# A routed expert layer and a gated recurrence on one core: gathers without pace, down products one unit sooner, and a new layout of the recurrence's pieces

## The reference

```python
shared = silu(xf @ w1) * (xf @ w3) @ w2
s = sigmoid(concat([xf, tf]) @ router_W)              # tf: cond, repeated over the tokens
topk_idx = top_k(s + router_bias, 2); gates = s of the two / their sum
y = gelu(xf @ W1e[e]) @ W2e[e]                        # for each expert e
x = x + (shared + sum of gates * y over the two) / 3
# then, from h = cond, for t in 0..255:
gate = sigmoid(h @ Wh.T + x[:, t] @ Wz.T + b)
h = tanh(h * (1 - alpha) + gate * x[:, t])
out[:, t] = x[:, t] + h
```

## Time and profile before

| | us |
|---|---|
| median of 3 runs | 763.66 |
| lowest, highest | 762.21, 768.95 |
| the profiled execution, its own time | 764.96 |
| its span, first to last instruction | 763.1 |

### The profile page before, as it was taken

One profiled execution on the slowest core, in us unless ns is written; L12 is line 12 of the kernel. 1 busy time (PEld: TensorE's weight loads), 2 busy tenths in 40 slices (PEclk: granted clock), 3 DMA queues, 4 the chain that ended last, 5 costly groups with the idle time before them and its releaser, 6 DMA issues.

```text
span 763.1 us, 22288 instructions
## 1 busy us (share of the span) xinstructions
PE 700.4 (92%) x8562; PEld 505.6 (66%) x8562; DVE 547.1 (72%) x2014; ACT 472.9 (62%) x1347; POOL 270.8 (35%) x284
## 2 busy tenths in 40 slices
PE   5899897998999999999999899999999999999763
PEld 3455486645888656898578786566889555686442
DVE  4887651457877698877688786898976678866854
ACT  4746473634677755777676577556877645676533
POOL 2037464265642156452174025773040173002100
PEclk9999998999999999999999999999999999999965
DMA  8836899893896785996869654366475354133101
GB/s 284 326 112 228 220 247 263 204 201 109 208 237 191 166 166 146 216 203 186 208 152 224 112 140 158 127 164 142 105 202 140 113 153 132 43 92 118 43 15 43
DMA packets 166460, 124.73 MB, mean 163 GB/s; under 512 B 118706, under 2 KB 147156, under 8 KB 166356
## 3 DMA queue, kind: packets, MB, share of 16 engines
q1 hardware_dynamic: 150436, 79.19, 44.7%
q0 software_dynamic: 14368, 41.96, 17.3%
q10 hardware_dynamic: 1552, 2.15, 0.8%
HBM read 39.90 MB, written 55.84 MB: 125 GB/s over the span
## 4 chain that ended last, share of the span: by engine, by line
PE 68%; DVE 15%; ACT 8%; DMA 4%; issue 3%; POOL 0%; ACTq 0%; DVEq 0%; POOLq 0%
PE bank L1739 64%; PE bank L1967 2%; DVE hid_low L1507 2%; DVE pre L1561 2%; DMA xe<-x_slots_even 2%; DVE taken L1558 2%; DVE full L1500 1%; PE bank L1902 1%; DMA y_got<-y_slots_even,where 1%; ACT th L1257 1%; ACT hs_high L1265 1%; DVE r_part L1522 1%; DVE r_sum L1526 1%; DVE left L1419 1%; DVE x_parts L1378 1%
## 5 line engine op out<-in xcount | busy, mean ns | idle before, releaser
L1739 PE MATMUL bank<-xe,w1e_high 128*128 128x128 f16 x1360 | 215.9, 221 | 9.5 <-DMA xe<-x_slots_even 5.9
L1739 PE MATMUL bank<-xs,w_high 128*128 128x512 f16 x512 | 167.3, 382 | 5.2 <-DVE w_low L1677 3.0
L1739 PE MATMUL bank<-xe,w1e_low 128*128 128x128 f16 x680 | 146.9, 221 | 1.1
L1739 PEld LDWEIGHTS bank<-xe,w1e_high 128*128 x1360 | 125.5, 99 | 20.9 <-issue 7.8
L1507 DVE TENSOR_TENSOR hid_low<-full,hid_high 128x512 f16<-128x512 f32 (+1 forms) x152 | 102.9, 677 | 49.2 <-ACT hid_high L1210 39.1
L1257 ACT ACTIVATE th<-bank 128x64 f32<-128x64 f32 x256 | 56.9, 222 | 93.3 <-PE bank L1739 89.5
L1265 ACT ACTIVATE hs_high<-pre 128x64 f16<-128x64 f32 x256 | 65.5, 256 | 73.1 <-DVE pre L1561 64.8
L1558 DVE SCALAR_TENSOR_TENSOR taken<-th,zq 128x64 f32<-128x64 f32 x256 | 57.9, 226 | 69.7 <-ACT th L1257 66.8
L1739 PEld LDWEIGHTS bank<-hs_high,gwt_high 128*128 128x128 f16 x1024 | 68.2, 97 | 51.8 <-ACT hs_high L1265 38.0
L1078 POOL TENSOR_TENSOR fence_pool<-zero 128x1 f32<-128x1 f32 x12 | 3.4, 280 | 274.7 <-DMA y_slots_odd<-y_pair 84.7
L1739 PE MATMUL bank<-hs_high,gwt_high 128*128 128x32 f16 x1024 | 79.1, 178 | 20.5 <-ACT hs_high L1265 20.0
(11 more groups left out here) (156 smaller groups left out, 1704.4 us busy)
## 6 DMA issues: line engine op xcount, KB each, us to landing
y_slots_even<-y_pair SPq DMA_DIRECT2D x45, 256.0 KB
y_slots_odd<-y_pair SPq DMA_DIRECT2D x37, 256.0 KB
x_res<-in_x_dram SPq DMA_DIRECT2D x16, 512.0 KB
out_dram<-o_tok SPq DMA_DIRECT2D x32, 256.0 KB, 3.5
x_tok<-in_x_dram SPq DMA_DIRECT2D x14, 512.0 KB
x_slots_even<-zeros POOLq DMA_DIRECT2D x1, 4096.0 KB, 18.1
x_slots_odd<-zeros POOLq DMA_DIRECT2D x1, 4096.0 KB, 15.0
y_got<-in_L_cond_W1e_dram SPq DMA_DIRECT2D x4, 512.0 KB, 13.9
```

Of the source, the lines that this page charges most:

```text
L1739: return pe.matmul(out_ap, w, mov, start=start, stop=stop, skip_group_check=True)
```

## The change

Nothing that is computed changes, and each engine's instructions stay the same in kind and number but for their waits. What changes is where they stand:

- GATHER_STEP of sections 3 and 4 is -1 throughout: no pace. (Section 2 keeps its own.) The last scatters of section 4 are paced by steps 109 to 134 where it was 112 to 143, those of section 5 by steps 149 to 154 where it was 163 to 170. GATHER_AT and SCATTER_AT move by some units; the gathers of section 3 begin one unit sooner in POOL's order, among the scatters of section 4.
- The down products of the units in SOON stand one unit after their up products, where it was two. Where a unit then has two, both are done, one behind the other; where it has none, it has none.
- act_residual follows: one unit sooner for groups 12 and 13.
- Group 12's second transposes (kc = 1) stand in the same unit 133 as its first, behind the down products (LATE). Before, they stood in 134 and 135.
- FINISH moves for group 12 (132 to 131), 13 (135 stays) and 14 (138 to 141). Group 15's four tiles are weighed in two units again, where it was one.
- OUT_AT moves some chunks by one to four units, for instance chunk 22 from 128 to 130.
- PE_AT, ACT_AT and DVE_AT are new from unit 42 on.

```diff
-FINISH = [FIRST_SHARED[_q] + GROUP for _q in range(N_GROUPS)]
-for _q, _u in enumerate((37, 40, 43, 61, 64, 67, 83, 86, 89, 104, 107, 111, 132, 135, 138, 151)):
-    FINISH[_q] = _u
-AT_ONCE = (15,)
-SUM_AT = {_q: [FINISH[_q] + 2 - (_q in AT_ONCE), FINISH[_q] + 3 - (_q in AT_ONCE)] for _q in range(N_GROUPS) if AHEAD[_q]}
...
+FINISH = [37, 40, 43, 61, 64, 67, 83, 86, 89, 104, 107, 111, 131, 135, 141, 151]
+AT_ONCE = ()
+SUM_AT = [[39, 40], [42, 43], [45, 46], [63, 64], [66, 67], [69, 70], [85, 86], [88, 89], [91, 92], [106, 107], [109, 110], [113, 114], [133, 133], [137, 138], [143, 145], [152, 153]]
+SOON = (100, 110, 128, 129, 131, 132, 133, 134, 135, 138, 150)
...
-SCATTER_AT = [[_f + _j * _a // _b for _j in range(_n)] for _n, _f, _a, _b in zip(
-    SECTIONS, (7, 18, 39, 63, 96, 118), (1, 1, 1, 1, 2, 1), (2, 1, 1, 1, 3, 1))]
-GATHER_AT = [[_f + _j * _a // _b for _j in range(_n)] for _n, _f, _a, _b in zip(
-    SECTIONS, (34, 58, 80, 100, 128, 148), (1, 1, 1, 1, 1, 1), (2, 2, 2, 2, 2, 2))]
+SCATTER_AT = [
+    [7, 7, 8, 8, 9, 9, 10, 10, 11, 11, 12, 12], [18, 19, 20, 21, 22, 23, 24, 25, 26, 27, 28, 29],
+    [39, 40, 41, 42, 43, 44, 45, 46, 47, 48, 49, 50], [63, 64, 65, 66, 67, 68, 69, 70, 71, 72, 73, 74],
+    [96, 96, 97, 98, 98, 99, 100, 100, 101, 102, 102, 103], [109, 110, 111, 112],
+]
+GATHER_AT = [
+    [34, 34, 35, 35, 36, 36, 37, 37, 38, 38, 39, 39], [58, 58, 59, 59, 60, 60, 61, 61, 62, 62, 63, 63],
+    [80, 80, 81, 81, 82, 82, 83, 83, 84, 84, 85, 85], [99, 99, 100, 100, 101, 101, 102, 102, 103, 103, 104, 104],
+    [135, 135, 136, 136, 137, 137, 138, 138, 139, 139, 140, 140], [147, 147, 148, 148],
+]
...
-    4: (112, 113, 114, 115, 116, 117, 118, 119, 120, 121, 122, 123, 126, 127, 128, 129, 132, 133, 136, 137, 138, 139, 142, 143),
-    5: (163, 164, 165, 166, 167, 168, 169, 170),
+    4: (109, 110, 111, 112, 113, 114, 115, 116, 117, 118, 119, 120, 123, 124, 125, 120, 123, 124, 127, 128, 129, 130, 133, 134),
+    5: (149, 150, 151, 152, 153, 154, 154, 149),
...
-    3: (123, 124, 125, 125, 129, 130, 131, 131, 133, 134, 135, 135, 139, 140, 140, 141, 143, 144, 144, 145, 146, 146, 147, 148),
-    4: (187, 187, 188, 188, 189, 189, -1, -1, 191, -1, -1, -1, -1, -1, -1, -1, -1, -1, -1, -1, -1, -1, -1, 192),
+    3: (-1, -1, -1, -1, -1, -1, -1, -1, -1, -1, -1, -1, -1, -1, -1, -1, -1, -1, -1, -1, -1, -1, -1, -1),
+    4: (-1, -1, -1, -1, -1, -1, -1, -1, -1, -1, -1, -1, -1, -1, -1, -1, -1, -1, -1, -1, -1, -1, -1, -1),
...
-    46: 0, 49: 1, 53: 2, 57: 3, 61: 4, 70: 5, 71: 6, 73: 7, 78: 8, 82: 9, 92: 10, 94: 11, 97: 12, 98: 13, 100: 14,
-    104: 15, 111: 16, 115: 17, 118: 18, 119: 19, 120: 20, 123: 21, 128: 22, 132: 23, 138: 24, 141: 25, 147: 26,
-    150: 27, 153: 28, 154: 29, 155: 30, 156: 31,
+    46: 0, 49: 1, 53: 2, 57: 3, 61: 4, 70: 5, 71: 6, 73: 7, 78: 8, 82: 9, 92: 10, 94: 11, 97: 12, 99: 13, 100: 14,
+    104: 15, 111: 16, 115: 17, 118: 18, 121: 19, 122: 20, 125: 21, 130: 22, 133: 23, 138: 24, 141: 25, 147: 26,
+    150: 27, 154: 28, 157: 29, 159: 30, 160: 31,
...
     assert _u not in MISC, (_u, _item)
     MISC[_u] = _item
-SPARE = [MISC[_u] for _u in sorted(MISC)]
+LATE = {_at[0]: (SUM, (_q, 1)) for _q, _at in enumerate(SUM_AT) if _at[1] == _at[0]}
+SPARE = [_at[_u] for _u in sorted(MISC) for _at in (MISC, LATE) if _u in _at]
+assert all(UNITS[_u].kind == SHARED == UNITS[_u + 1].kind for _u in SOON)
...
 
+        def down_at(i):
+
+            return i + DOWN_LAG - (i in SOON)
+
...
-                    if u.i == (FIRST_SHARED[q] + MID + DOWN_LAG if AHEAD[q] else max(FIRST_SHARED[q] + MID, FINISH[q]) + 2):
+                    if u.i == (down_at(FIRST_SHARED[q] + MID - 1) + 1 if AHEAD[q] else max(FIRST_SHARED[q] + MID, FINISH[q]) + 2):
...
-                        if AHEAD[q] and u.i == SUM_AT[q][kc]:
+                        if AHEAD[q] and u.i == SUM_AT[q][kc] and (kc == 0 or u.i not in LATE):
                             add_part(q, kc)
                             gap()
                 gap()
                 if u.kind == SHARED:
                     product(u)
+                if u.i in LATE:
+                    gap()
+                    add_part(*LATE[u.i][1])
...
                         turn_tokens(q)
-                pair_down, shared_down = units_at(u.i - DOWN_LAG, EXPERT), units_at(u.i - DOWN_LAG, SHARED)
-                if shared_down and u.kind != SHARED:
-                    down_shared(shared_down, gap)
+                pair_down = units_at(u.i - DOWN_LAG, EXPERT)
+                shared_downs = [units_at(i, SHARED) for i in range(u.i - DOWN_LAG, u.i)
+                                if units_at(i, SHARED) and down_at(i) == u.i]
+                if shared_downs and u.kind != SHARED:
+                    down_shared(shared_downs[0], gap)
                 gap()
                 if u.kind == EXPERT:
...
+                    for v in shared_downs:
+                        if v is not shared_downs[0]:
+                            gap()
+                        down_shared(v, gap)
                     gap()
+                if u.i in LATE:
+                    misc(*LATE[u.i], gap)
```

The tables where the steps of group 12 begin and where the ordinary work ends, PE's part:

```diff
...
-    (131, 2): ((HIGH, 188),), (131, 3): ((STEP, 188),), (131, 10): ((HIGH, 189),), (131, 11): ((STEP, 189),),
-    (132, 0): ((HIGH, 190),), (132, 1): ((STEP, 190),), (132, 8): ((HIGH, 191),), (132, 9): ((STEP, 191),),
...
-    (136, 7): ((FILL, 48), (FILL, 49), (HIGH, 192), (STEP, 192),), (136, 14): ((HIGH, 193), (STEP, 193),),
...
-    (151, 18): ((HIGH, 231), (STEP, 231), (FILL, 58), (FILL, 59), (HIGH, 232), (STEP, 232),),
-    (152, 5): ((HIGH, 233), (STEP, 233),), (152, 7): ((HIGH, 234), (STEP, 234), (HIGH, 235),), (152, 9): ((STEP, 235),),
-    (153, 5): ((HIGH, 236), (STEP, 236), (HIGH, 237),), (153, 6): ((STEP, 237),),
...
+    (132, 8): ((HIGH, 187), (STEP, 187),), (132, 16): ((HIGH, 188), (STEP, 188),), (132, 25): ((HIGH, 189),),
+    (133, 1): ((STEP, 189),), (133, 11): ((HIGH, 190), (STEP, 190),), (133, 21): ((HIGH, 191), (STEP, 191),),
+    (134, 11): ((FILL, 48), (FILL, 49), (HIGH, 192), (STEP, 192), (FILL, 50), (FILL, 51), (HIGH, 193), (STEP, 193),),
+    (134, 17): ((HIGH, 194),), (134, 18): ((STEP, 194),), (135, 7): ((HIGH, 195), (STEP, 195),),
...
+    (151, 14): ((HIGH, 231),), (151, 15): ((STEP, 231), (FILL, 58), (FILL, 59), (HIGH, 232), (STEP, 232),),
+    (151, 20): ((HIGH, 233),), (151, 21): ((STEP, 233),), (151, 26): ((HIGH, 234),), (152, 0): ((STEP, 234),),
+    (152, 3): ((HIGH, 235),), (152, 5): ((STEP, 235),), (153, 5): ((HIGH, 236), (STEP, 236), (HIGH, 237),),
+    (153, 6): ((STEP, 237),), (154, 0): ((HIGH, 238), (STEP, 238),),
...
```

More of the change, by code:

```diff
@@ L358 @@
+    (159, 5): ((GATE, 251), (STATE, 251), (GATE, 252),),
+    (160, 4): ((STATE, 252), (GATE, 253), (STATE, 253), (GATE, 254),), (161, 3): ((STATE, 254),),
+    (161, 4): ((GATE, 255),), (161, 5): ((STATE, 255),),
 }
 DVE_AT = {
[L360 to L362 removed]
@@ new lines @@
+    (54, 5): ((MIX, 26),), (54, 8): ((REST, 26),),
+    (56, 2): ((MIX, 27), (REST, 27), (MIX, 28), (REST, 28), (MIX, 29), (REST, 29), (MIX, 30),), (56, 3): ((REST, 30),),
+    (56, 7): ((MIX, 31),), (57, 2): ((REST, 31),), (57, 10): ((MIX, 32),), (57, 11): ((REST, 32),),
+    (57, 13): ((MIX, 33),), (58, 2): ((REST, 33),), (58, 7): ((MIX, 34),), (58, 9): ((REST, 34),),
+    (58, 11): ((MIX, 35),), (59, 2): ((REST, 35),), (59, 7): ((MIX, 36),), (60, 1): ((REST, 36),),
+    (60, 7): ((MIX, 37),), (60, 10): ((REST, 37),), (61, 0): ((MIX, 38),), (61, 2): ((REST, 38),),
@@ new lines @@
+    (61, 4): ((MIX, 39),), (61, 8): ((REST, 39),), (61, 12): ((MIX, 40),), (61, 14): ((REST, 40),),
+    (61, 16): ((MIX, 41),), (62, 2): ((REST, 41),), (62, 4): ((MIX, 42),), (62, 9): ((REST, 42),),
+    (62, 10): ((MIX, 43),), (63, 1): ((REST, 43),), (63, 3): ((MIX, 44),), (63, 8): ((REST, 44),),
+    (63, 9): ((MIX, 45),), (64, 0): ((REST, 45), (MIX, 46),), (64, 1): ((REST, 46),), (64, 2): ((MIX, 47),),
+    (64, 3): ((Z, 6),), (64, 5): ((REST, 47),), (65, 2): ((MIX, 48),), (65, 4): ((REST, 48),),
@@ new lines @@
+    (105, 2): ((REST, 132),), (105, 4): ((MIX, 133),), (105, 5): ((REST, 133),),
+    (105, 10): ((MIX, 134), (REST, 134), (MIX, 135),), (106, 1): ((REST, 135),), (106, 2): ((MIX, 136),),
+    (106, 4): ((REST, 136),), (106, 5): ((MIX, 137),), (106, 7): ((REST, 137),), (107, 1): ((MIX, 138),),
+    (107, 2): ((REST, 138),), (107, 3): ((MIX, 139),), (107, 4): ((REST, 139),), (107, 6): ((MIX, 140),),
+    (107, 8): ((REST, 140), (Z, 18),), (107, 9): ((MIX, 141),), (108, 1): ((REST, 141),), (108, 2): ((MIX, 142),),
@@ new lines @@
+    (119, 3): ((REST, 164),), (119, 4): ((MIX, 165),), (119, 7): ((REST, 165),), (120, 2): ((MIX, 166),),
+    (120, 4): ((REST, 166),), (120, 8): ((MIX, 167),), (121, 2): ((REST, 167),), (121, 6): ((MIX, 168),),
+    (121, 9): ((REST, 168),), (122, 0): ((MIX, 169),), (122, 3): ((REST, 169),), (122, 6): ((MIX, 170),),
+    (122, 7): ((REST, 170), (MIX, 171),), (123, 0): ((REST, 171),), (123, 5): ((MIX, 172),),
```

(11 more changed lines are left out.)

682 lines of the change are left out of this document (325 added, 357 removed).

## The result

The changed kernel takes 755.54 us (median of 4 runs, 753.18 to 757.93) where the kernel before takes 763.64 us (4 runs beside it, 762.21 to 768.95). The ratio is 0.9882, with a 95% interval of 0.9849 to 0.9915: 1.2% faster. A second set of 6 runs gave 753.99 us and 0.9863 (0.9823 to 0.9903). The forecast was 762.2 us with a range down to 756.0, so it missed the time by 6.7 us, and what came was the outcome "faster by over 1%", to which it gave a chance of 0.10.

A forecast was written before the change was run, and what follows sets the result against it. PE's own queue was taken as the bound up to about 714.5 us, then the recurrence's chain. Terms -1.5 - 0.7 + 0.7 = -1.5 us, taken off the median of 763.66 us, gave 762.2 us; range 756 to 769.

The forecast's parts named there:

- faster by over 1%: Outcome below 756.0 us, needing the lead kept and more, or unseen savings before unit 100; chance 0.10.
- the recurrence stands still there, PE doesn't: On the 18.39 us hole between the states of steps 191 and 192: PE is full in it.
- wider spacing: Steps from 192 on, spread over the closed hole, save PE's waits for a state: -0.7 us, between 0 and -1.6.
- The step fewer at the end: One step more is done before PE's ordinary work ends: 1 x 1.50 = -1.5 us, bounds 0 and -7.5.
- Down products: Moved one unit sooner at eleven units, PE waits briefly for hid_low at units 100 and 128: +0.7 us with chunk 22.
- second rival: Down products come too early, each of the eleven costing 1.0 us: +8.8 us in sum, 772.5 us; chance 0.09.
- The zeros: The terms put at 0 us: gathers and scatters, act_residual with group 12's transposes, and everything before unit 100.
- Gathers and scatters: POOL's gathers without pace and sooner scatters, sections 3 to 5: 0 us, bounds 0 and +4.2.
- act_residual and the transposes of group 12: Group 12's z two units forward, with add_part waiting on DVE around units 133 and 134: 0 us, up to +0.5.
- Before unit 100: Pieces laid anew by up to a unit or two, in both directions: 0 us, between -2 and +2.
- The chain keeps its lead: Rival: steps after 192 hold its lead to unit 151's end, 4 more steps done, 756.2 us; chance 0.12.
- collision with the gathers: Rival: an unpaced transfer lands in 7.06 us instead of 2.90, +4.2 us on the forecast, 766.4 us; chance 0.07.

The follow-up runs named there:

- again: A second profile of the changed kernel, with nothing altered; its runs took 753.99 us, ratio 0.9863 to the kernel before.
- e2: The changed kernel with group 11's load of x_res issued two units sooner; 754.74 us, ratio 0.9851 to the kernel before.
- e7: Kernel before with the changed kernel's pieces of steps 0 to 191, chunks 13 and 19 to 23 moved, gathers without pace, down products unmoved; 769.86 us.
- e18: e7 with the down products of the units in SOON also one unit sooner; 765.75 us, ratio 1.0028 to the kernel before.
- spaced runs: PE's pieces of steps 48 to 231 moved by at most 0.5 us: kernel before 767.43 us (770.84 with ACT and DVE following), changed kernel 758.24 us.

## Why the prediction was wrong

**What bounds the kernel.** Right in its two regimes: the cadence at the end is unchanged, and PE's queue is the bound until then. Wrong in the sentence "the recurrence stands still there, PE doesn't", and in "all of PE's waits for a state in this stretch are 1.6 us", taken as what wider spacing could save at most. That is the step that failed. The earlier trace rows list only what goes beyond the modelled end of the product ahead; from start to start PE lost 6.61 + 1.53 + 4.11 us in units 111 to 148 alone. The changed kernel gets 3.8 us of these back in the profile shown, 6.1 us in "again", and 5.9 us in e2, where the stall isn't there. Not 0.7 us, and well outside 0 to 1.6.

**The step fewer at the end, -1.5 us.** It is there, and it shortens the part behind the first long wait: last state less first long wait is 756.82 - 715.42 = 41.40 us before and 749.32 - 709.76 = 39.56 us after, 1.84 us. But from the turning of chunk 27 on, at 708.69 and 701.79 us in the two kernels, PE needs 6.73 us to that wait before and 7.97 us after, since more of the steps' products stand there now. Net the tail loses 0.6 us less in this pair. The mechanism was right, its size here less than half. In the executions in which the old order's last down products meet the lower clock (four of the eight profiles with the old end) the difference is 1.7 to 2.2 us; that part wasn't forecast.

**Down products, +0.7 us.** The term can't be read as a number of its own. Alone the edit costs 6.4 us, over half of what the second rival gives it, by another mechanism than the one that it names; with steps laid for it, PE waits for hid_low once, 0.7 us, and the moved products cover steps 186 to 191 (the same steps without them: e7). Adding up the parts of this change, each priced against the old order, was itself a mistake: 5.5 and 6.4 us alone are 3.1 us together.

**The zeros.** Gathers and scatters: shown for the gathers (0.9996 alone). The rule that the forecast quoted from the Trainium skill, page "DMA: Bandwidth & Descriptors", "Queues, rings and completion order", would have made the sum 4.2 us higher; of the gathers without pace no run shows such a cost. Sooner scatters were not tried alone. act_residual and the transposes of group 12: not tried alone; zq is waited for 0.5 us, as before. Before unit 100: the new pieces to step 90 gave 0.9967, about 2.6 us, a little past the bound of 2, with an interval that reaches almost to nothing.

**The rivals.** "The chain keeps its lead" named 756.2 us, close to the time, but not what happened: only one step fewer is left, not four more. Step 192's lead of 10.36 us (634.84 to 624.48) is 7.50 us at the last state, which is simply the amount by which everything, PE's ordinary work too, is sooner. No collision with the gathers was seen. What was late is a load of x_res behind xe in SP's own queue; PE's wait for it is 1.0 to 3.4 us in six profiles, and by the medians its worth can't be told.

What is shown: where the gain is. It is in short gaps of PE that the page counts as busy, 2.9 us of it at units 131 to 148 in each of the three profiles of the changed kernel (after, again, e2), and 0.9 to 3.2 us at units 111 to 131; the 3.15 us at units 43 to 90 in the pair shown can't be told from what varies by itself. It is also shown that the parts don't add: the new pieces up to step 191 and the moved products each make the kernel slower alone (5.5 and 6.4 us), are still 3.1 us slower together, and the changed kernel with the old pieces is slower too.

What stays open is which property of the new orders does it, and which of the edits between e18 and the changed kernel carry the last 1.5%: steps 192 to 255, the sums, the chunks, and POOL's order were only ever changed together. Even spacing in PE's order isn't it. That a shifted step meets other work of ACT or DVE fits the spaced runs, but it was argued from single steps, not tested by itself.

## What to carry to other kernels

When an engine's queue is the bound, measure its lost time from start to start against the usual interval of each kind of instruction; a list of waits, and "busy" too, can hide most of it where ends are modelled. When orders on three engines are laid by hand or by a planner, an edit of one item in them is worth what it is worth with the rest laid for it, so price the layout as a whole and don't add up parts. A rule that sorts a handful of finished layouts rightly can still fail as a recipe: try it as an edit before it is believed.

## What the runs showed of the hardware that was not expected

PE's lost time in a stretch with a fixed order repeats to 0.02 us between executions and even between kernels (2.12 to 2.14 us in units 138 to 148 of five profiles, 4.11 to 4.13 us in five others), while the whole time varies by some us from run to run. What varies is a few longer stalls, at the start and where a load or a gather lands late, and whether the last down products of the old order meet the lower clock (1.1 to 1.5 us in step 235).

One such stall also slows what follows. The windows of the changed kernel around the wait in unit 111 (columns as in the earlier trace rows):

```profile
520.00:525.00 5.00, 2.19 (x9) 0.84 (x10) 2.65 (x10) 0.63 (x3) 0.00 (x0) 0.59 0.30 111
525.00:530.00 5.00, 5.00 (x60) 3.79 (x59) 2.71 (x10) 1.48 (x5) 0.00 (x0) 0.72 0.00 0
```

The granted clock is 0.59 in the 5 us with the wait and still 0.72 in the next 5 us, in which PE is busy throughout: between the two levels of 2.4 and 1.2 GHz it spends more than half of those 5 us at the lower one. The products of 512 columns behind the wait start 0.43 us apart instead of 0.215. A stall of 3.4 us so costs more than itself: step 150 to step 151 lost 4.98 us in that profile.
